# Two attention stages on one core: three in eight key tiles get the logarithm of their weight in the score bank ahead of the products, and the causal diagonal of the maxima moves from TensorE to VectorE

## The reference, cut to what matters

```python
# first attention ("prior"): softmax over the listed keys, or over all keys with a bias
lam = 10.0 * exp(-5.0 * u_prev);  use_sparse = lam >= 1.0         # one flag for each batch
scores = einsum('bhqd,bhkd->bhqk', Q, K) * scale
dense_out = softmax(scores + lam * where(prior_mask, 0.0, -1.0)) @ V
s_scores = where(prior_index_mask, Q . K[prior_indices], -inf)    # 32 listed keys a query
out = where(use_sparse, softmax(s_scores) @ V[prior_indices], dense_out)
# second attention ("causal"): on the result of the first
attn = softmax(where(tril, q @ k.T * scale, -inf));  y = attn @ v
```

## Time and profile before

| | |
|---|---|
| median of 3 runs | 1667.64 us (1666.7 to 1669.23) |
| span of the profiled execution | 1660.4 us, 20515 instructions |
| PE busy | 1558.2 us (94%), 7392 matmuls |
| DVE busy | 869.0 us (52%) |
| ACT busy | 734.8 us (44%) |
| POOL busy | 696.3 us (42%) |
| granted TensorE clock, mean | 0.964 of full |

### The profile page before, as it was taken

The page is one execution under the profiler, slowest core; times in us unless marked ns, Lnnn a source line. Parts: engine busy times, 40 slices in busy tenths (PEclk is TensorE's granted clock), DMA queues, the critical chain, the costliest instruction groups (busy, mean ns, idle before and its releaser), DMA issues. The chain is left out here.

```text
span 1660.4 us, 20515 instructions
## 1 busy us (share of the span) xinstructions
PE 1558.2 (94%) x7392; PEld 762.5 (46%) x7392; DVE 869.0 (52%) x2041; ACT 734.8 (44%) x998; POOL 696.3 (42%) x515
## 2 busy tenths in 40 slices
PE   5789999989999999899999888999999999999998
PEld 3423333323333333333433334555656577777755
DVE  7578878888678855557765733342422111111141
ACT  4754666766566665476645566223211111111111
POOL 4437999987799998143210120400001200000070
PEclk9559999999999999999998898999999999999999
DMA  3551033243231310344532015100040005243071
GB/s 97 143 155 33 24 80 76 70 98 78 60 85 35 79 46 8 79 117 109 125 73 64 28 33 166 61 0 0 0 152 4 22 1 183 92 162 114 16 129 24
DMA packets 75905, 121.43 MB, mean 73 GB/s; under 512 B 14920, under 2 KB 53265, under 8 KB 72731
## 3 DMA queue, kind: packets, MB, share of 16 engines
q1 hardware_dynamic: 72155, 113.62, 24.3%
q0 software_dynamic: 3072, 6.03, 2.1%
q10 hardware_dynamic: 576, 0.47, 0.1%
HBM read 85.08 MB, written 36.96 MB: 74 GB/s over the span
## 5 line engine op out<-in xcount | busy, mean ns | idle before, releaser
L1141 POOL TENSOR_TENSOR sb_prob<-sb_prob,sb_weight 128x1024 f32<-128x1024 f32 x192 | 448.0, 2357 | 44.6 <-ACT sb_prob L1355 44.1
L1355 ACT ACTIVATE sb_prob<-wide 128x1024 f32<-128x1024 f32 (+3 forms) x384 | 347.5, 916 | 207.9 <-PE wide L1965 109.1
L1960 PE MATMUL wide<-sb_stack_q,sb_stack_k 99*128 99x512 bf16 (+3 forms) x896 | 282.8, 364 | 16.2 <-ACT sb_prob L1355 7.4
L1399 ACT ACTIVATE sb_sil<-wide 128x320 f32<-128x320 f32 (+1 forms) x128 | 66.2, 517 | 436.0 <-PE wide L2039 436.0
L1644 DVE CUSTOM_DVE_ANT_0 sb_junk<-bank,sb_bias 128x512 bf16<-128x512 f32 x339 | 226.8, 688 | 61.7 <-PE bank L1933 57.0
L1933 PE MATMUL bank<-sb_stack_k,sb_stack_q 96*128 96x512 bf16 (+3 forms) x597 | 217.3, 380 | 17.1 <-DVE sb_rowmax L1638 5.8
L2039 PE MATMUL wide<-sb_weight,sb_ffn 128*128 128x512 f32 x512 | 232.3, 597 | 0.0
L1980 PE MATMUL wide<-sb_prob,sb_v_aug 128*17 128x512 f32 (+3 forms) x1792 | 221.2, 560 | 7.6 <-ACT sb_o_raw L1368 6.2
L1638 DVE TENSOR_REDUCE sb_rowmax<-bank 128x1 f32<-128x512 f32 (+3 forms) x258 | 139.2, 559 | 88.3 <-PE bank L1936 57.1
L1771 DVE TENSOR_TENSOR sb_act_s<-sb_sil,wide 128x512 f32<-128x512 f32 x64 | 43.9, 687 | 253.3 <-ACT sb_sil L1399 253.3
L1179 POOL DMA_INDIRECT sb_weight<-slots_out,sb_slot_r x32 | 31.5, 984 | 285.0 <-issue 283.2
(11 more groups left out here) (272 smaller groups left out, 1831.7 us busy)
## 6 DMA issues: line engine op xcount, KB each, us to landing
sb_stack_k<-parts SPq DMA_DIRECT2D x32, 256.0 KB, 6.8
o_raw<-sb_o_raw SPq DMA_DIRECT2D x32, 256.0 KB, 2.3
sb_big<-rg SPq DMA_DIRECT2D x8, 1024.0 KB, 4.9
sb_big<-ru SPq DMA_DIRECT2D x8, 1024.0 KB, 7.3
sb_big<-rd SPq DMA_DIRECT2D x8, 1024.0 KB, 10.7
sb_stack_q<-parts SPq DMA_DIRECT2D x16, 384.0 KB, 4.9
parts<-sb_o_norm SPq DMA_DIRECT2D x40, 128.0 KB
sb_stack_q<-parts SPq DMA_DIRECT2D x16, 256.0 KB, 5.4
```

The source lines that it names most:

```text
L1141: e.tensor_tensor(p, p, weight_of(*u[1:]), ALU.mult).then_inc(weigh_p.handle, 1)
L1355: e.activation(p[:, :, first:HALF], sc[:, :, first:HALF], ACT.Exp).then_inc(SC.empty_sem(u), 1)
L1399: e.activation(sil[:, i % 2, 0:n], SC.tile(u)[:, 0:n], ACT.Silu).then_inc(silu_a.handle, 1)
L1960: i = e.matmul(sc[:, j * HALF + first:(j + 1) * HALF], stack_k[0:ROWS_M, n % 3, g, kt * P:(kt + 1) * P], stack_q[0:ROWS_M, n % 3, g, half ...
```

## The change

**Logarithms in the bank.** `POOL_UNITS` goes; `LOGGED = (1, 4, 6)` names key tiles instead, so 12 of a prior job's 32 units are "filled" and 20 go to GpSimd (before: 24 to GpSimd, 8 to VectorE). For each logged key tile, half and batch (12 in all) ScalarE replaces the weight by its logarithm with a tiny bias (step "log"), and VectorE adds -1e30 for unlisted keys (step "bar"). For a filled unit ScalarE first copies the logarithms into the wide buffer, for both heads (step "fill"), TensorE adds the scores on top (`start=False`), and ScalarE takes the exponential to `prob`. No product with `cut`, no multiplication on GpSimd or VectorE. The fill of a unit stands one unit early in the plan, ahead of the exponential of the unit before it.

**The causal diagonal.** The 256 products with `neg_qk` go. The causal maxima that touch the diagonal are taken with the custom instruction, which adds a constant row (`above`: zeros, then the triangle) from SBUF. The remaining changes make room: `flags` and `keep` move into other tensors, the constants come in two transfers, and two small memsets are added.

```diff
-POOL_UNITS = (0, 1, 3, 4, 5, 7)
+LOGGED = (1, 4, 6)
...
 def to_pool(n, u):
-    return JOBS[n][0] == 0 and u % 8 in POOL_UNITS
+    return JOBS[n][0] == 0 and not to_fill(n, u)
+def to_fill(n, u):
+    return JOBS[n][0] == 0 and place(n, u)[1] in LOGGED
...
+    for i, (b, t, half) in enumerate(rows):
+        if t in LOGGED:
+            tables[i + 1].append(("log", b, t, half))
+            (tables[i + 2] if i + 2 < len(tables) else tables[i + 1]).append(("bar", b, t, half))
...
+        if i + 1 < len(queue) and to_fill(*queue[i + 1]):
+            plan.append(("fill", *queue[i + 1]))
         if i < len(queue):
             plan.append(("score", n, u))
-        if 0 < i <= len(queue):
-            m, v = queue[i - 1]
-            if JOBS[m][0] == 0 and not to_pool(m, v):
-                plan.append(("weigh", m, v))
...
+                    late += [(i + 7, ("log", 1, kt, half)), (i + 8, ("bar", 1, kt, half))] if kt in LOGGED else []
...
+                elif kind == "fill":                                       # ScalarE
+                    w.wait_ge(weight_ready(*u[1:]))
+                    w.wait_ge(SC.vacant(key_))
+                    e.activation(heads_of(SC.tile(key_)[:]), weight_of(*u[1:]), ACT.Copy).then_inc(fill_a.handle, 1)
+                elif kind == "log":
+                    w.wait_ge(weight_made(b, t, half))
+                    e.activation(o, o, ACT.Ln, bias=least).then_inc(log_a.handle, 1)
...
+                    if att:                                                # VectorE, maxima
+                        e.tensor_tensor_reduce(
+                            out=junk[:, i % 2, 0:hi - lo], in0=BK.tile(u)[:, 0:hi - lo], in1=above[:, HALF - (hi - lo):],
+                            scale=1.0, scalar=-3e38, op0=ALU.add, op1=ALU.max, accum_out=acc).then_inc(BK.empty_sem(u), 1)
...
+                elif kind == "bar":
+                    e.scalar_tensor_tensor(out=weight[:, t, cols], in0=unlisted[:, t, cols], scalar=fl[5][:, b:b + 1],
+                                           in1=weight[:, t, cols], op0=ALU.mult, op1=ALU.add).then_inc(bar_d.handle, 1)
...
-                    if diag:                                               # TensorE, maxima
-                        i = e.matmul(bk[:, hi - lo - P:hi - lo], C["ident"], C["neg_qk"], start=False, stop=True)
...
-                    w.wait_ge(SC.vacant(u))
+                    w.wait_ge(fill_a.after(u[1:]) if to_fill(n, v) else SC.vacant(u))
...
-                                     start=True, stop=not to_pool(n, v))
+                                     start=not to_fill(n, v), stop=not to_pool(n, v), skip_group_check=to_fill(n, v))
```

More of the change, by code:

```diff
@@ L84 @@
 CB_W = 6 * P
+CB_AT = dict(ident=0, neg_qk=HALF, before=HALF + P, ones=HALF + 2 * P, iota=HALF + 3 * P)
 JOBS = [(att, b, q) for att, b in ((0, 0), (0, 1), (1, 0), (1, 1)) for q in range(NQ)]
@@ L550, in build @@
         cf = sb("const_f32", [P, P + 2 * E])
-        cb = sb("const_bf16", [P, CB_W], BF16)
+        cb = sb("const_bf16", [P, 2 * HALF], BF16)
         F = dict(ident=cf[:, 0:P], iota_e=cf[:, P:P + E], slot_e=cf[:, P + E:P + 2 * E])
-        C = {k: cb[:, a:a + n] for k, (a, n) in CB.items()}
+        C = {k: cb[:, a:a + P] for k, a in CB_AT.items()}
+        above = cb[:, P:P + HALF]
+        keep = C["iota"]
         xT = sb("xT", [P, DC, T])
@@ L775, in build @@
         top_a = signal("act_top", [u for u in of("fin") if u[2] % 2])
-        exp_a = signal("act_exp_wide", [u for u in of("score") if JOBS[u[1]][0] == 0 and not to_pool(*u[1:])])
+        log_a = signal("act_log", [u[1:] for u in of("log")])
+        bar_d = signal("dve_bar", [u[1:] for u in of("bar")])
+        fill_a = signal("act_fill", [u[1:] for u in of("fill")])
         weigh_p = signal("pool_weigh", [u[1:] for u in of("score") if to_pool(*u[1:])])
@@ L827, in weight_ready @@
             half, kt, _ = place(n, u)
-            return weight_made(JOBS[n][1], kt, half)
+            return bar_d.after((JOBS[n][1], kt, half)) if to_fill(n, u) else weight_made(JOBS[n][1], kt, half)
         def weight_made(b, kt, half):
@@ L1097, in _ @@
             e.memset(rowmax[:], -3e38).then_inc(const_done.handle, 1)
+            w.wait_ge(const_done.after("rowmax"))
+            e.memset(above[:, 0:HALF - P], 0.0).then_inc(const_done.handle, 1)
+            w.wait_ge(const_done.after("zeros"))
+            e.memset(least, LEAST).then_inc(const_done.handle, 1)
             w.wait_ge(const_done.end)
@@ L1132, in _ @@
                 elif u == ("zero", 0):
-                    w.wait_ge(SC.emptied([v for v in of("score") if JOBS[v[1]][0] == 0][-1]))
+                    w.wait_ge(SC.emptied(PRIOR_LAST))
                     e.memset(zeros, 0.0).then_inc(zeroed.handle, 1)
@@ L1355, in _ @@
                     e.activation(p[:, :, first:HALF], sc[:, :, first:HALF], ACT.Exp).then_inc(SC.empty_sem(u), 1)
+                elif kind == "fill":
+                    key_ = ("score", *u[1:])
+                    w.wait_ge(weight_ready(*u[1:]))
+                    w.wait_ge(SC.vacant(key_))
+                    e.activation(heads_of(SC.tile(key_)[:]), weight_of(*u[1:]), ACT.Copy).then_inc(fill_a.handle, 1)
+                elif kind == "log":
+                    _, b, t, half = u
+                    o = weight[:, t, half * HALF:(half + 1) * HALF]
+                    w.wait_ge(const_done.end)
+                    w.wait_ge(weight_made(b, t, half))
+                    e.activation(o, o, ACT.Ln, bias=least).then_inc(log_a.handle, 1)
                 elif kind == "turn":
@@ L1670, in _ @@
                     e.tensor_tensor(o, BK.tile(u)[:], o, ALU.add).then_inc(BK.empty_sem(u), 1)
[L1671 to L1680 removed]
+                elif kind == "bar":
+                    _, b, t, half = u
+                    cols = slice(half * HALF, (half + 1) * HALF)
+                    w.wait_ge(log_a.after(u[1:]))
+                    w.wait_ge(unlisted_a.after((0, t, half)))
+                    e.scalar_tensor_tensor(out=weight[:, t, cols], in0=unlisted[:, t, cols], scalar=fl[5][:, b:b + 1],
+                                           in1=weight[:, t, cols], op0=ALU.mult, op1=ALU.add).then_inc(bar_d.handle, 1)
                 elif kind in MIX_KINDS:
@@ L1926, in _ @@
                     _, n, h, qt, half = u
-                    causal = JOBS[n][0]
-                    lo, hi = half * HALF, min((half + 1) * HALF, (qt + 1) * P if causal else S)
-                    diag = causal and hi == (qt + 1) * P
+                    lo = half * HALF
+                    hi = lo + max_width(u)
                     bk = BK.tile(u)
```

42 lines of the change are left out of this document (17 added, 25 removed).

## The result

The changed kernel takes **1694.52 us** (median of 4 runs, 1688.4 to 1704.13), the kernel before 1667.17 beside it (1666.67 to 1669.23): a ratio of **1.0165, 95% interval 1.0131 to 1.0198**. It is slower by 27 us; the forecast was 4 faster, and its range ended at 1686. The profiled execution spans 1686.7 us against 1660.4.

A forecast was written before the change was run, and what follows sets the result against it. The prediction took TensorE and GpSimd, both nearly full and in balance, to bound the prior stage. Relief of -14.1, -12, -12, -4, -4 and costs of +30, +6, +6 summed to -4.1, so 1663.5 us, range 1642 to 1686.

The forecast's parts named there:

- ScalarE's chain becomes the bound: Rival, 26%: in filled pairs of prior jobs, ScalarE's in-order work reaches TensorE; copies and logarithms cost 58 us, giving 1685.
- copies: Prior stage: 96 ScalarE copies into two wide buffers make TensorE wait; +30 us, bounds 0 to 67.
- logarithms in jobs 3 and 4: Six logarithms, each with two table loads, 3.2 us of ScalarE's queue, some 2 us slack; +6 us, between 0 and 19.
- start: Ahead of the first unit: six bars between VectorE's maxima, a table reload and a late last bar; +6 us (3 to 11).
- VectorE's multiplication, maxima behind it: Prior stage: TensorE's 17.0 us of waits for the multiplication mostly go, -12; maxima queued behind it come free earlier, -4.
- products with the cut, GpSimd: Prior stage: 64 fewer TensorE products, -14.1 us; GpSimd's 75 us less work removes most of TensorE's 7.7 wait, -4.
- diagonal products: 256 TensorE products go, 15.4 us, about 50 of them in the prior stage; VectorE's exchange taken as zero; -12 us.
- the chain: Filled pairs on two wide buffers: copies and exponentials alternate on ScalarE; the second unit waits 0.7 us, the first does not.
- its sign of being wrong, 45: The prediction called itself wrong if the scores' waits for copies exceeded 45 us or stayed below 15.
- the balance that the prediction's first part describes: Prior stage: TensorE 437 and GpSimd 453 of 537 us, so relieving one alone gives little.

The follow-up runs named there:

- square of four runs: The changed kernel with or without its 96 copies and the logarithms' table loads; prior stage 563.1 us, no loads 548.2, no copies 526.7, neither 511.2.
- the diagonal part alone: Kernel before with only the causal diagonal moved from TensorE to VectorE, without logarithms, bars or copies: ratio 0.9969 to the kernel before.
- evenly placed units with the value products three behind: Changed kernel, filled units 2, 4, 7, 9, 11 and 13 of sixteen, value products three units behind the scores instead of four: ratio 1.0207 to the kernel before.
- the woven order: Changed kernel with the two pairs of heads of neighbouring key tiles in turn in the prior jobs; output incomplete: ratio 1.0311 to the kernel before, prior stage 586.5 us.

## Why the prediction was wrong, by its steps

**The case that came in is the rival "ScalarE's chain becomes the bound"**, with the place it named (filled pairs, ScalarE in order) and the point from which it decides: copies and logarithms over 40 us. They cost 52. I gave it 26% and 1685; measured 1694.5. The forecast's sum of -4.1 missed by 31, and no step alone did it. Half of the miss is cost: copies, logarithms and start were put at 42 us and came to 59. The other half is relief: 46 us were counted and 28 came. That half is also why the time is above the rival's 1685, although its costs, 58 us for copies and logarithms, were above the measured 52. The two steps that failed most are the logarithms and VectorE's multiplication, 9 to 10 us each. (The measured terms add up to +31 for the 27 of the whole.)

| term | predicted | measured | by |
|---|---|---|---|
| copies | +30 | +37 | square of four runs |
| logarithms in jobs 3 and 4 | +6 | +15 | the same square |
| start | +6 | +7.0 | first score, after |
| VectorE's multiplication, maxima behind it | -12 - 4 | -6.5 | that multiplication left out |
| products with the cut, GpSimd | -14.1 - 4 | -16.6, with up to 3 of the diagonal in it | rest of the relief |
| diagonal products | -12 | -5.2 | the diagonal part alone |

*The logarithms* are the step that failed most for its size. I let 2 of the 3.2 us of each hide in slack, because ScalarE needs 1 us of every 2.1. The slack hid only a quarter: 6 x 3.28 = 19.7 us of ScalarE became 15 of the stage. It isn't the copies that took the slack, since the loads cost as much without them, 15.5 us. A visit delays whatever stands behind it in order, on more engines than ScalarE. At the one that begins at 403.87:

```profile
405.92 0.75 DVE L1710 SCALAR_TENSOR_TENSOR sb_weight<-sb_unlisted,sb_tiny,sb_weight 128x512 f32<-128x512 bf16 x1 [2.21 <-ACT sb_weight L1383]
407.42 0.38 PE L1939 MATMUL bank<-sb_y_prior,sb_const_bf 128*128 128x512 bf16 x1 [1.41 <-DVE sb_rowmax L1678]
410.07 0.39 PE L1963 MATMUL wide<-sb_stack_k,sb_stack_q 96*128 96x512 bf16 x1 [2.27 <-ACT sb_mrow L1389]
```

VectorE waits 2.21 us for the logarithm with its step "bar", the maxima stand behind that, and TensorE waits 1.41 us for a maximum; then it waits 2.27 us for a row of maxima that ScalarE copies out only after its two late exponentials. The prediction counted ScalarE's queue alone, and not VectorE's behind the bar. TensorE's granted clock has a part in it too. The stretch 370 to 455, which holds the six late logarithms, in the kernel after and without the table loads:

```profile
370.00:455.00 85.00, 73.09 (x354) 24.98 (x353) 59.05 (x162) 76.53 (x85) 48.00 (x23) 0.94 0.25 64
```

```profile
370.00:455.00 85.00, 79.59 (x413) 28.38 (x413) 67.80 (x189) 69.28 (x82) 59.71 (x27) 1.00 0.31 78
```

354 matmuls against 413 in the same 85 us, and a clock of 0.94 against 1.00: TensorE was granted its lower level, 1.2 GHz, for some 10 us of the stretch. Over each run's own prior stage the time at that level is 27 us after the change and 24 without copies, and 7 in both runs without table loads. By one execution of each, it goes with the loads and not with the copies (the kernel before has 10). As work at half the clock takes at most twice as long, an estimate of its part is at most 5 us in this stretch and 10 in the stage. The prediction had no term for that.

By the 2.66 us a switch of the Trainium skill, page "ScalarE: Activation LUTs", section "What ACT_TABLE_LOAD costs", the six would have held ScalarE 5.9 us each, an estimate. The trace disagrees: the kernel after shows loads of 1.28 us that start 0.02 us after the instruction before, as the earlier trace rows did, so my miss isn't a drain that the trace hides:

```profile
403.05 0.80 ACT L1351 ACTIVATE sb_weight<-sb_y_prior,sb_tiny 128x512 f32<-128x512 uint8 x1
403.87 1.28 ACT L1383 ACT_TABLE_LOAD   x1
405.16 0.72 ACT L1383 ACTIVATE sb_weight<-sb_weight,sb_tiny 128x512 f32<-128x512 f32 x1
...
405.90 1.28 ACT L1372 ACT_TABLE_LOAD   x1
407.19 1.94 ACT L1372 ACTIVATE sb_prob<-wide 128x1024 f32<-128x1024 f32 x2
```

*The copies*: the chain was right (first unit of a pair free, second late), as was their duration (1.03 for 1.02). In the pair shown the second unit waits 0.48 where 0.7 was computed, but over 48 pairs 37 us came out, 0.77 a pair for 0.62. The told wait of 25 to 45 us on about 40 occasions is 33.1 on 45 by the matmuls, and 58.6 on 53 by the weight loads. The first lies within the range told, the second beyond its sign of being wrong, 45. The term's size is off by 7. What I missed is that it was a choice of the order: with the value products one unit earlier less than half of these waits are left by the matmuls, 21 for 45.

*VectorE's multiplication*: 17.0 us of waits for it were taken almost as gain. Without it TensorE and GpSimd are still at 519 and 495 of 540 us, so most of these waits became others: in the same window those of the scores for the exponential grew from 6.6 to 13.3 us, and those of the value products for GpSimd from 7.7 to 10.9. It gave 6.5 of 16. This is the balance that the prediction's first part describes and its sum didn't use. The 16.6 us of the rest show the counterpart: taken together, products and GpSimd gave nearly what was counted.

*The diagonal products*: the matmuls are gone, 15.4 us by the earlier trace rows, but 5.2 came out, by the ratio of that part alone. I bounded VectorE's exchange by zero. The instruction itself did exchange evenly (0.553 us for 0.554 at 384 columns, 0.421 for 0.421 at 256), but it brings a read of the accumulator that the plain reduction hasn't, here for the causal stage in the run with the diagonal part alone:

```profile
L1683 DVE DVE_READ_ACCUMULATOR2_ANT sb_rowmax<- 128x1 f32 x207 | 17.2, 83 | 0.1
```

In the causal stage TensorE's weight loads of the maxima wait for VectorE 19.7 + 10.6 us before, and in that run:

```profile
PEld bank L1983 <- DVE sb_rowmax L1683: 11.4, 23, 1.6
PEld bank L1983 <- DVE sb_rowmax L1677: 10.8, 15, 2.7
PEld wide L1983 <- DVE sb_rowmax L1683: 8.3, 15, 2.0
PEld wide L1983 <- DVE sb_rowmax L1677: 7.9, 7, 2.8
```

That is 38.4 us for 30.3. The rest of the difference fits the granted clock (0.93 there, 0.95 before), which I can't separate with these runs.

*What held*: over its prior stage GpSimd is at 416 us (below 430), VectorE at 354 (below 360) and ScalarE at 433 (430 to 450), the start cost 7.0 for 6 (it doesn't hang on the table loads: 127.9 without them), and the copy takes 1.0 us. *What didn't*: a prior stage of 530 to 540 (563.1), a causal stage shorter by 8 to 14 (5.6).

*What stays open*: why copies on evenly placed units with the value products three behind (558.4) cost more than in pairs (541.7); in both orders that parted the pairs and lost, most filled units stand two apart and so share one wide buffer, which wasn't tested by itself. Open too are why three behind lengthens VectorE's chain so much, and what the woven order leaves out.

## What to carry to other kernels

Where an operation is put in front of a product in a ring of two buffers, its price is the wait that the ring can't cover; count the work that the bound engine has between two refills, and put other work (here the value products) exactly there before judging the idea: it took 21 us off the stage and 13 off the whole time, and without the copies the same shift cost 9. Take waits for an engine as gain only after asking which wait comes next, above all where two engines are nearly full: 17 us of waits gave 6.5. And a rare long visit in an in-order queue, such as a table load on either side of a logarithm, can cost most of its length (15 of 20 us here, with copies in the queue or without): follow what stands behind it on every engine that waits for it.

## What the runs showed of the hardware

A copy of 128 x 1024 floats from SBUF to PSUM takes ScalarE 1.03 us and VectorE 1.22. A shift of TensorE's work by one unit, with the same instructions, moved one stage by -21, +9 and +27 us in three kernels. In all three the causal stage grew too (361.2 to 369.0, 365.3 to 369.4, 366.8 to 369.4), and so did what follows it (636.2 to 640.9, 640.5 to 645.9, 639.4 to 645.5). So 9 to 13 us were added outside the stage that the shift aims at, in profiles of one execution each; the execution of the kernel after was a quick one, so its 13 may be too large. The time at TensorE's lower clock in the prior stage went with the table loads and not with the copies, in one execution each: 27 and 24 us with the loads, 7 and 7 without.
